# One run of nine projection matmuls, fixed banks, and two rounding steps on GpSimd

## What is computed

```python
def _layer(x, wqkv, qs, ksc, wo, lg, lb, w1, b1, w2, b2):
    h = shift_token(x)                      # upper 64 channels one token later
    q, k, v = jnp.split(h @ wqkv, 3, axis=-1)      # 8 heads of 64
    q = l2norm(q) * qs
    k = l2norm(k) * ksc
    q, k = rotary_xpos(q, k)
    o = local_attention(q, k, v)            # windows of 64, one window back
    x = x + o @ wo
    h = shift_token(x)
    h = (h - mu) / jnp.sqrt(var + 1e-05) * lg + lb
    h = h @ w1 + b1
    a, g = jnp.split(h, 2, axis=-1)
    return x + (a * gelu(g)) @ w2 + b2
```

## Time and profile before

| what | us |
|---|---|
| three runs, median (range) | 1446.06 (1443.96 to 1450.64) |
| the profiled execution, whole | 1446.23 |
| its span on the core | 1444.4 |
| busy: PE / PEld | 1330.5 (92%) / 982.3 (68%) |
| busy: ACT / DVE / POOL | 1156.2 (80%) / 1140.5 (79%) / 955.2 (66%) |
| PE in 200 to 300 us (layer 0 attention) | 96.92 of 100 |
| PE in 900 to 1000 us (layer 1 attention) | 93.27 of 100, DVE 85.20, ACT 88.26, POOL 81.70 |
| granted TensorE clock, both stretches | 1.00 |

### The profile page before, as it was taken

The page is one execution under the profiler, slowest core; times in us unless marked ns, Lnnn a source line. Parts: engine busy times, 40 slices in busy tenths (PEclk is TensorE's granted clock), DMA queues, the critical chain, the costliest instruction groups (busy, mean ns, idle before and its releaser), DMA issues.

```text
span 1444.4 us, 37742 instructions
## 1 busy us (share of the span) xinstructions
PE 1330.5 (92%) x13656; PEld 982.3 (68%) x13656; DVE 1140.5 (79%) x1944; ACT 1156.2 (80%) x3542; POOL 955.2 (66%) x616
## 2 busy tenths in 40 slices
PE   3899999999999998999979999999999999998997
PEld 2677777777777776655557777777777777776664
DVE  5877888788878775587788888888888888874787
ACT  4889999989998887454478888888888888887754
POOL 2778887887788786111178888888888888872110
PEclk9999999999999999899999999999999999999999
DMA  5222222222222211020011111111111111110223
GB/s 153 49 57 62 65 66 62 63 57 64 57 60 49 49 39 27 15 58 1 1 39 42 42 42 41 41 41 41 41 42 41 39 41 42 35 42 23 59 73 87
DMA packets 60600, 70.33 MB, mean 49 GB/s; under 512 B 8961, under 2 KB 38529, under 8 KB 60417
## 3 DMA queue, kind: packets, MB, share of 16 engines
q1 hardware_dynamic: 60416, 67.93, 19.7%
HBM read 13.40 MB, written 4.19 MB: 12 GB/s over the span
## 4 chain that ended last, share of the span: by engine, by line
ACT 33%; PE 33%; DVE 16%; issue 14%; POOL 2%; DMA 1%; ACTq 1%; SPq 0%; DVEq 0%; POOLq 0%
PE ps L165 30%; ACT P L571 14%; DVE nm L847 4%; ACT sqk L545 4%; ACT Vn L585 3%; DVE t L828 3%; PE ps L201 2%; ACT oT L601 2%; ACT qT L592 2%; ACT PT L561 2%; DVE ss L837 2%; ACT side L486 1%; DVE sq L882 1%; POOL t L1065 1%; DVE side L748 1%
## 5 line engine op out<-in xcount | busy, mean ns | idle before, releaser
L571 ACT ACTIVATE P<-ps,nm 128x128 f32<-128x128 f32 x1024 | 358.6, 375 | 77.4 <-DVE nm L847 77.1
L1065 POOL TENSOR_TENSOR P<-P,rden 128x512 f32<-128x512 f32 x256 | 266.7, 1044 | 203.3 <-DVE rden L854 203.3
L165 PE MATMUL ps<-wqkv,hT 128*128 128x512 f32 x1152 | 338.8, 421 | 45.6 <-POOL hT L1065 25.3
L1065 POOL TENSOR_TENSOR t<-t 128x1024 f32<-128x1024 f32 x128 | 331.0, 2586 | 29.9 <-DVE t L828 29.9
L823 DVE TENSOR_TENSOR t<-ps,tabl 128x1024 f32<-128x1024 f32 x128 | 156.4, 1222 | 157.3 <-ACT sqk L545 157.3
L165 PEld LDWEIGHTS ps<-wqkv,hT 128*128 128x128 f32 x1152 | 199.8, 191 | 115.2 <-POOL hT L1065 29.6
L1065 POOL TENSOR_TENSOR t<-t,rr 128x1024 f32<-128x1024 f32 x128 | 244.9, 1913 | 12.8 <-ACT rr L554 3.1
L571 ACT ACTIVATION_READ_ACCUMULATOR P<-ps,nm 128x1 f32 x1024 | 220.0, 215 | 0.0
L847 DVE TENSOR_REDUCE nm<-ps 128x4 f32<-128x512 f32 x256 | 174.3, 682 | 21.2 <-PE ps L165 21.0
L1065 POOL TENSOR_TENSOR hnr<-B,hnr 128x512 fp32r<-128x512 f32 x32 | 41.6, 1301 | 204.8 <-ACT hnr L609 204.8
L828 DVE TENSOR_TENSOR t<-ps,tabl 128x512 f32<-128x512 f32 x256 | 173.4, 679 | 0.5 <-POOL t L1065 0.5
(11 more groups left out here) (120 smaller groups left out, 2427.1 us busy)
## 6 DMA issues: line engine op xcount, KB each, us to landing
Vs<-Vn SPq DMA_DIRECT2D x224, 128.0 KB, 2.3
side<-in_x SPq DMA_DIRECT2D x16, 256.0 KB, 3.4
hsh<-X SPq DMA_DIRECT2D x32, 128.0 KB, 2.3
A<-X SPq DMA_DIRECT2D x16, 256.0 KB, 2.4
h<-X SPq DMA_DIRECT2D x32, 128.0 KB, 2.2
oT<-in_x SPq DMA_DIRECT2D x16, 256.0 KB, 3.0
out<-oT SPq DMA_DIRECT2D x16, 256.0 KB, 2.4
hsh<-X SPq DMA_DIRECT2D x32, 127.8 KB, 2.4
```

Of the source, the lines that this page charges most:

```text
L165: return e.matmul(o, lhsT, rhs, start=start, stop=stop, skip_group_check=True)
L571: k = act(P[:, g, :], ps[:, 3 + s, (g % 4) * 128:(g % 4 + 1) * 128], ACT.Exp, bias=nm[:, g:g + 1], accum_out=den[:, g:g + 1])
L1065: return e.tensor_tensor(o, a, b_, op)
```

## The change

It does five things.

1. `v_proj(l, i+1)` stands right behind `qk_proj(l, i+1)`: nine matmuls in a run. Bank 7 holds V and then the attention output; bank 2 holds all side products.
2. The side product of an iteration moves from its end to between `attend` and `turn_qk`. `attend` waits only for `keep_v`; a function `side_free` waits, ahead of the next side product, for what emptied bank 2. `v_proj` waits for `keep_o` of the tile attended in the same iteration.
3. On ScalarE `keep_v` moves to the head of the iteration, `keep_o` ahead of `keep_q`, and `root_var` from the start of B to the end of A, ahead of `square`.
4. `ln_apply` and the rounding of `hT` move from ScalarE to GpSimd (`tensor_scalar`); the latter stands with the remainder in `shift_split`.
5. On VectorE `centre` and `proj_add` stand at the head of an iteration, ahead of `rotate(i, 0)`.

```diff
         def tensor(e):
             def v_proj(l, i):
...
-                product(ps[:, vbank(i), :], b, t, 2).then_inc(s_vm, 1)
+                if i == 0:
+                    e.wait_ge(s_wlo, 4 * l + 3)
+
+                if i >= 4:
+                    e.wait_ge(s_o, n - 3)
+                elif i:
+                    e.wait_ge(s_v, n)
+                product(ps[:, 7, :], b, t, 2).then_inc(s_vm, 1)
+
+            def side_free(l, i):
+
+                if (b := hit(i, 5)) is not None:
+                    e.wait_ge(s_xadd, 2 * (l * NB + b) + 1)
+                elif (b := hit(i, 7)) is not None:
+                    e.wait_ge(s_xadd, 2 * (l * NB + b) + 2)
+                elif (b := hit(i, 8)) is not None:
+                    e.wait_ge(s_hc, l * NB + b + 1)
+                elif (b := hit(i, 10)) is not None:
+                    e.wait_ge(s_rv, l * NB + b + 1)
...
-                else:
-                    e.wait_ge(s_v, n + 3)
+                if i + 3 < NT:
+                    e.wait_ge(s_v, n + 4)
+                else:
+                    e.wait_ge(s_o, n)
...
                     if i + 1 < NT:
                         qk_proj(l, i + 1)
...
+                        v_proj(l, i + 1)
         def gpsimd(e):
...
-            def shift_lo(l, b):
-                e.wait_ge(s_hi, l * NB + b + 1)
+            def ln_apply(b):
+                xb = tiles(xr[b % 2])
+                e.wait_ge(s_nmr, b + 1)
+                if b:
+                    e.wait_ge(s_tx, b)
+                for t in range(TPB):
+                    k = e.tensor_scalar(xnb[:, t * 128:(t + 1) * 128], xb[:, t, :], rst[:, t:t + 1], nmr[:, t:t + 1],
+                                        ALU.mult, ALU.add)
+                k.then_inc(s_nrm, 1)
+
+            def shift_split(l, b):
+                m = l * NB + b
+                e.wait_ge(s_hsh, 32 * (m + 1))
+                if m > 1:
+                    e.wait_ge(s_vm, 4 * m - 4)
+                e.tensor_scalar(hT[:, b % 2, 0, :], hsh[:, b % 2, :], 1.0, 0.0, ALU.mult, ALU.add).then_inc(s_hi, 1)
+                e.wait_ge(s_hi, m + 1)
                 tt(hT[:, b % 2, 1, :], hsh[:, b % 2, :], hT[:, b % 2, 0, :].bitcast(F32), ALU.subtract).then_inc(s_h, 1)
...
                 for i in range(NT + 3):
+                    if l == 0 and (b := hit(i, -6)) is not None and b > 1:
+                        ln_apply(b)
                     if 0 <= i - 2 < NT:
                         normalise(l, i - 2, 0)
```

More of the change, by code:

```diff
@@ L377, in tensor @@
                         turn_p(l, i - 3)
[L378 to L387, removed]
-                        else:
[L389 to L394, removed]
+                    extra = False
@@ new lines, in tensor @@
+                    if l == 0:
+                        b = 1 if i == 1 else hit(i, -5)
+                        if b is not None and b >= 1:
+                            e.wait_ge(s_x, b)
+                            side_free(l, i - 1)
+                            ln_turn(b, 2)
+                            extra = True
+                    elif (b := hit(i, 6)) is not None:
+                        side_free(l, i - 1)
+                        rec_out(b, 2)
+                        extra = True
@@ L407, in tensor @@
                     if 0 <= i - 3 < NT:
                         attend(l, i - 3)
+                    if i >= 5:
+                        if not extra:
+                            side_free(l, i - 1)
+                        elif l == 0:
+                            e.wait_ge(s_x, hit(i, -5) + 1)
+                        else:
+                            e.wait_ge(s_osq, hit(i, 6) + 1)
+                    if (b := hit(i, 8)) is not None:
+                        if l == 0 and b == 0:
+                            e.wait_ge(s_wts, 48)
+                        mean(l, b, 2)
@@ new lines, in tensor @@
+                    if (b := hit(i, 5)) is not None:
+                        e.wait_ge(s_o, l * NT + 4 * b + 2)
+                        if l == 0 and b == 0:
+                            e.wait_ge(s_wts, 48)
+                            e.wait_ge(s_x, 2)
+                        proj(l, b, 0, 2)
+                    if (b := hit(i, 7)) is not None:
+                        e.wait_ge(s_o, l * NT + 4 * b + 4)
+                        proj(l, b, 1, 2)
+                    if (b := hit(i, 10)) is not None:
+                        var(l, b, 2)
@@ L412, in tensor @@
                         qk_proj(l, i + 1)
[L413 to L425, removed]
-                        e.wait_ge(s_o, l * NT + 4 * b + 2)
-                        if l == 0 and b == 0:
-                            e.wait_ge(s_wts, 48)
-                        proj(l, b, 0, vbank(i))
-                    if (b := hit(i, 7)) is not None:
-                        e.wait_ge(s_o, l * NT + 4 * b + 4)
-                        proj(l, b, 1, vbank(i))
-                    if (b := hit(i, 10)) is not None:
-                        var(l, b, vbank(i))
+                        v_proj(l, i + 1)
                     if i == NT + 2:
@@ L639, in scalar @@
             ln_root(0)
-            ln_apply(0)
             for c in range(2):
@@ L668, in scalar @@
                             ln_root(b)
-                        if (b := hit(i, -6)) is not None and b > 1:
-                            ln_apply(b)
                     else:
```

112 lines of the change are left out of this document (36 added, 76 removed).

## The result

The changed kernel is slower: 1482.95 us median of four executions (1475.22 to 1483.71) against 1446.07 for the kernel before, a ratio of 1.0239 with a 95% interval of 1.0197 to 1.028, which is clear of no change. The prediction was 1442 us in a range of 1399 to 1462. The profiled execution took 1483.1 us, its span 1481.3, at a mean granted TensorE clock of 0.965 (before: 0.990).

The account below looks back on a forecast made before the run. The prediction took layer 0 as bound by TensorE's own work and layer 1 as having larger holes. From 1446.2 us, -13 (layer 0), +11 (layer 1) and -2 (start) gave 1442 us, range 1399 to 1462.

Parts of the forecast that it names:

- The V matmuls in the run: TensorE, every tile: three V matmuls take 0.74 us in the run against 0.89 in their own slot, 0.15 less.
- root_var ahead of PT: First two tiles of a cycle: `attend` waits for PT; they take 17.94 us in layer 1, 17.09 in layer 0.
- Rounding on GpSimd: GpSimd: rounding `hT` takes 0.8 us and `ln_apply` 1.6; in layer 1 GpSimd is just in time for the run.
- mean in layer 1: TensorE in C: `mean` waits for the copy of X, starting at 6.7 us, not 3.27; cycle +0.72, 15 cycles +11.
- mean in layer 0: TensorE in C: wait for `h` of 0 to 0.7 us, taken as 0.4; the whole cycle -0.92, 14 cycles -13.
- The ends of the layers and the feed-forward stages: Outside the steady cycles: no separate term for layer ends; feed-forward stages 0, since TensorE does not wait for ScalarE there.
- The start: Kernel's start: GpSimd can begin the first rounding 3 us earlier than ScalarE; between 0 and -2.8, taken as -2 us.
- The rivals: Three alternatives: VectorE's root ahead of GpSimd's add (0.20), GpSimd as limit (0.15), no gain from the nine-matmul run (0.08).
- the rival: Layer 1, VectorE: L718 (L748 before) runs ahead of GpSimd's add, 0.29 us long; C 8.0, total 1400; chance 0.20.
- GpSimd as the bound: GpSimd: `ln_apply` and rounding together over 3.4 us make `hT` late in layer 0; total 1469 us; chance 0.15.

Follow-up runs that it names:

- warm1: Changed kernel plus three matmuls (result overwritten) ahead of `mean`'s wait for `h`, in layer 1 alone: 1457.4 us, ratio 1.0077 to the kernel before.
- x_first0: Changed kernel with X's second half ahead of `scale_hc` on VectorE, in layer 0 alone: 1471.7 us, ratio 1.0163 to the kernel before.
- rr_only: Changed kernel with layer 1's `rec_root` moved from B's end into C and `rec_root2` behind C's `square`: 1447.3 us, ratio 0.9998 to the kernel before.
- root_back: Changed kernel with `root_var` back behind the K copy on ScalarE in layer 1: 1473.6 us, ratio 1.0185 to the kernel before.
- x_first: Changed kernel with X's second half directly behind the K copies on VectorE, in both layers: 1433.9 us, ratio 0.9922 to the kernel before.
- mean_late: Changed kernel with `mean` moved behind `v_proj`, to the iteration's end: 1457.4 us, ratio 1.0072 to the kernel before.
- gp_alone: Kernel before with only `ln_apply` and the rounding of `hT` moved to GpSimd (one wait added): 1457.2 us, ratio 1.0073 to the kernel before.

## Why the prediction was wrong, step by step

- **The V matmuls in the run**: right. From the first of the nine to the next `turn_p` it is 2.19 us in B and D. It is 2.33 in A of layer 1, and 2.75 at the median in C of layer 1, behind the stall; in `warm1` that C has 2.19. B and D in the packed form were 8.22 by the sum, and D is 8.07.
- **root_var ahead of PT**: right in size and place. `attend` in B at +3.67 and +3.51 (forecast about 3.7 in both layers), A and B 17.80 in layer 1 (17.94) and 16.9 in layer 0 (17.09).
- **Rounding on GpSimd**: 0.62 us instead of the 0.8 taken, next to the lower of its two rows (0.61 and 1.27); `ln_apply` took 4 x 0.46 us for the 1.6 taken. The remainder ends 15.5 after A's start instead of 15.71.
- **mean in layer 1**: `mean` starts 6.71 after C's start (forecast 6.7), L718 starts 0.51 behind the add (0.5). The term that failed is the one after it, "C = 6.7 + 0.96 + 2.38 + 0.74 = 10.78". It adds, behind a stall of 3.4 us, slots read at the full clock. The failed step is that no term stands for the clock. Behind the stall the granted clock is at its lower level, and C is 12.23 on the mean. With the hole filled (`warm1`) C is 10.54 and layer 1 takes 26 us less; 26 of the 41 us by which the total is off are in layer 1.
- **mean in layer 0**: the wait "0 to 0.7; I take 0.4" was mis-sized. The chain put X up to 0.7 behind C's start, but left `scale_hc` at its 0.9. Behind GpSimd's add it takes 2.27; the wait is then 1.9 and in some C's the clock falls too. It also took 2.3 us for every landing of the copy, where six of 14 took 2.8 to 4.1: the waits come to 0 to 3.3, and layer 0 has 17 us at the lower clock where before had none. With X ahead of it, layer 0 takes 12.6 us less (`x_first0`). The Trainium skill ("SBUF — State Buffer", section "SBUF: two separate sides") names operations of VectorE with two inputs from SBUF beside the copies as taking the shared ports, and I had carried over only the copies; the trace agrees, with 2.27 against 0.93.
- **The ends of the layers and the feed-forward stages** were put at nothing beyond the cycles. The last C of layer 0, at tile 61, has `mean` 6.6 after its start. Stage 0 gained 4.4, and had 13.7 us less at the lower clock; what brought the clock down there in the one kernel and not in the other was not tried.
- **The start**: -3.4 against -2 (0 to -2.8). Three kernels with the same code up to there (`warm1`, `rr_only`, `root_back`) have -2.2 to -3.0, so this term was about right.
- **The rivals**: L718 did not get ahead of the add by itself. Taken out of its way (`rr_only`), it took 0.42 us, where the rival had 0.29, and C became 8.15 at the median, where the rival had 8.0; the price of `rec_root2` in D is what the rival would not have had. GpSimd as the bound did not come: `ln_apply` and rounding take 2.5 us together, under the 3.4 from which it would decide. None of the rivals held the lower clock, and the range ended at 1462 because of it.

## What to carry to other kernels

When a matmul that waits for a transfer is moved ahead of others, price the wait by the whole chain that ends in the transfer, and price what follows at the lower clock where the profile of the new order would show a stall like this one: here the second price was 26 us, and all else in layer 1 came to 10. Price the landing by its spread and not by its median, once nothing hides it any more. Before shifting the waiting step, look for the instruction upstream that is held up by another engine's instruction (here L718, 2.59 us behind the add and 0.42 away from it), and move that one to a place where the other engine is idle. Two limits that stand within some hundredths of a microsecond of each other hide each other: an experiment that lifts one shows nothing, and both must be lifted together.

## What the runs showed of the hardware

- A stall of 3.4 us in each C (period 38 us) brought the granted clock to its lower level in each of the 13 C's of layer 1 that had it, 0.93 to 0.96 on the mean of 100 us between 900 and 1300 us. In `x_first`, waits of 0.34 and 1.26 us in each C left it at 1.00. In `mean_late` waits of 1.35 and 1.58, and in `gp_alone` one of 1.82 behind a shorter one, brought it down in 11 and in 9 of 14 cycles. In layer 0 of the changed kernel waits of 1.87 to 1.97 did so in three C's and not in a fourth (tile 13, 1.88), and a wait of 3.26 (tile 61) did not. What exactly decides between these is open.
- GpSimd's `tensor_scalar` on 128x512 took 0.62 us, as long as ScalarE's copy of the same tile (0.61 to 0.62), and half of its own two-operand form (1.27).
- VectorE's `scale_hc`, with two inputs from SBUF, took 2.27 us when GpSimd's add had begun 0.71 ahead of it (changed kernel), and 1.93 when it had begun 1.04 ahead (`x_first`, layer 0): it ended 0.54 to 0.55 behind the add's end either way. It took 0.93 where the add began 0.34 behind it, and 0.68 where both began together (`x_first`, layer 1). The add took 2.43 in the first two cases, and 2.8 to 2.9 in the last two.
- The second shifted copy of X (`h<-X`) landed 2.3 us behind its issue in most cycles and 2.5 to 4.4 in others, in the kernel before (5 of 14 in layer 1) as in `rr_only` (6 of 14).
